# Causal attention, 32 heads of 16: value products of four heads in one run, scores alternating with the maxima's pieces, and the maxima's mask on VectorE

## What is computed

```python
q = (x @ Wq.T + bq).reshape(b, l, h, hd).transpose(0, 2, 1, 3)   # b=2, l=1024, h=32, hd=16
k = (x @ Wk.T + bk).reshape(b, l, h, hd).transpose(0, 2, 1, 3)
v = (x @ Wv.T + bv).reshape(b, l, h, hd).transpose(0, 2, 1, 3)
scores = jnp.einsum('bhqd,bhkd->bhqk', q, k) / math.sqrt(hd)
scores = jnp.where(jnp.tril(jnp.ones((l, l), bool)), scores, -jnp.inf)
att = jax.nn.softmax(scores, axis=-1)
out = jnp.einsum('bhqk,bhkd->bhqd', att, v)
```

## Time and profile before

| | us |
|---|---|
| median of three runs | 4538.52 |
| profiled execution, its own time | 4516.65 |
| span of the profiled execution | 4514.9 |
| TensorE busy / VectorE busy | 4124.7 / 2840.9 |
| ScalarE busy / GpSimd busy | 1448.6 / 1940.0 |
| mean granted TensorE clock, share of full speed | 0.929 |

### The profile page before, as it was taken

One profiled execution on the slowest core, in us unless ns is written; L12 is line 12 of the kernel. 1 busy time (PEld: TensorE's weight loads), 2 busy tenths in 40 slices (PEclk: granted clock), 3 DMA queues, 4 the chain that ended last, 5 costly groups with the idle time before them and its releaser, 6 DMA issues.

```text
span 4514.9 us, 60472 instructions
## 1 busy us (share of the span) xinstructions
PE 4124.7 (91%) x18820; PEld 2878.9 (64%) x18820; DVE 2840.9 (63%) x4778; ACT 1448.6 (32%) x2386; POOL 1940.0 (43%) x1951
## 2 busy tenths in 40 slices
PE   7999979969999999989779999799699999999797
PEld 5443457747777777767654434677477777777676
DVE  3545444458888888874444553444588888888744
ACT  1233421143444444332113333211434444443321
POOL 1111233246666666654311111332466666666543
PEclk9888989979999999999988888899799999999999
DMA  2211011010011100001121210110100111010011
GB/s 69 34 34 29 13 36 42 21 35 27 26 33 33 30 28 28 22 18 42 39 70 34 34 29 13 36 42 21 36 29 24 33 33 30 28 30 23 16 42 40
DMA packets 80968, 145.11 MB, mean 32 GB/s; under 512 B 16152, under 2 KB 18056, under 8 KB 80784
## 3 DMA queue, kind: packets, MB, share of 16 engines
q1 hardware_dynamic: 80784, 142.84, 12.0%
HBM read 112.64 MB, written 4.19 MB: 26 GB/s over the span
## 4 chain that ended last, share of the span: by engine, by line
PE 70%; issue 10%; DVE 9%; POOL 4%; ACT 3%; DVEq 2%; POOLq 1%; SPq 1%; DMA 0%; ACTq 0%
PE banks L489 13%; PE banks L490 12%; PE banks L491 12%; PE banks L671 7%; PE banks L654 4%; PE banks L626 4%; PE banks L833 4%; DVE conv L1327 3%; PE banks L826 2%; PE banks L844 2%; PE banks L630 2%; PE banks L533 1%; POOL wg_lo L1589 1%; ACT conv L1004 1%; DVEq L1330 1%
## 5 line engine op out<-in xcount | busy, mean ns | idle before, releaser
L1224 DVE TENSOR_REDUCE mx<-banks 128x1 f32<-128x512 f32 (+3 forms) x768 | 408.2, 555 | 333.2 <-PE banks L630 225.1
L1327 DVE SCALAR_TENSOR_TENSOR conv<-banks,cpar,conv 128x509 f32<-128x509 f32 (+2 forms) x576 | 428.1, 744 | 88.1 <-ACT conv L1004 73.1
L1564 POOL TENSOR_SCALAR_AFFINE_SELECT probs<-probs 128x256 f32<-128x256 f32 x256 | 103.9, 407 | 802.2 <-ACT probs L947 800.7
L947 ACT ACTIVATE probs<-banks 128x1024 f32<-128x1024 f32 (+3 forms) x384 | 295.5, 809 | 476.5 <-PE banks L654 475.9
L1162 DVE TENSOR_TENSOR Y<-banks,Y 128x512 f32<-128x512 f32 x400 | 275.6, 692 | 232.4 <-PE banks L491 232.2
L626 PE MATMUL banks<-stack_k,stack_q 48*128 48x512 f32 (+3 forms) x768 | 344.9, 475 | 19.6 <-DMA stack_k<-part_hi 9.4
L1480 POOL TENSOR_SCALAR f_hi<-f_raw 128x512 fp32r<-128x512 f32 x150 | 93.6, 624 | 582.5 <-PE banks L491 472.3
L671 PE MATMUL banks<-probs,V 128*17 128x512 f32 (+3 forms) x1536 | 339.5, 561 | 0.7 <-POOL probs L1564 0.5
L626 PEld LDWEIGHTS banks<-stack_k,stack_q 48*128 48x128 f32 x768 | 152.0, 207 | 293.7 <-DVE mx L1224 172.7
L489 PE MATMUL banks<-xhi,f_hi 128*128 128x512 f32 x800 | 328.6, 411 | 3.6 <-DVE xlo L1133 3.6
L489 PE MATMUL banks<-xhi,wx_hi 128*128 128x512 f32 x768 | 312.4, 407 | 14.2 <-DVE conv L1327 14.2
(11 more groups left out here) (205 smaller groups left out, 9982.9 us busy)
## 6 DMA issues: line engine op xcount, KB each, us to landing
m_raw<-in_w_mamba SPq DMA_DIRECT2D x224, 256.0 KB, 2.7
f_raw<-in_w_ffn SPq DMA_DIRECT2D x50, 768.0 KB, 4.6
stack_q<-part_hi SPq DMA_DIRECT2D x128, 64.0 KB, 2.4
stack_k<-part_hi SPq DMA_DIRECT2D x128, 64.0 KB, 2.5
X<-in_x SPq DMA_DIRECT2D x4, 1024.0 KB, 6.5
wqk_raw<-in_w_attn SPq DMA_DIRECT2D x8, 512.0 KB, 3.6
stack_q<-part_lo SPq DMA_DIRECT2D x64, 64.0 KB, 2.4
stack_k<-part_lo SPq DMA_DIRECT2D x64, 64.0 KB, 2.4
```

The lines of the kernel that those rows point to most:

```text
L947: act.activation(probs[n % 2][:, 2 * p:2 * p + 2, 0:w], banks[:, 2 * p:2 * p + 2, 0:w], ACT.Exp, scale=1.0 / HD ** 0.5).then_inc(exp_done[ ...
L1224: dve.tensor_reduce(mx[:, s, h * TT + i:h * TT + i + 1], bank[RING_BANKS[ring % 3]][:, 0:cols], AX.X, ALU.max).then_inc(ring_free, 1)
L1327: r = dve.scalar_tensor_tensor(out=rest, in0=src[:, 0:HALF - lag], scalar=cpar[:, o:o + 1], in1=rest, op0=ALU.mult, op1=ALU.add)
```

## The change

The scores of a step are issued head by head with one piece behind each, and the values of the step before are one item of four heads behind the fourth piece (`values`, one wait for both pairs). The mask product on TensorE goes. In its place VectorE reads the piece with one instruction that adds `mask_qk` (now fp32, 128 x 512, zero but for its last 128 columns), writes the sum back to the bank and keeps the maximum. `mask_qk` is built by GpSimd at the start of each batch's attention.

```diff
                 for n in range(NS):
-                    for q in range(4):
-                        if q < 2:
-                            yield "scores", t, n, q
-                        elif n > 0:
-                            yield "values", t, n - 1, q - 2
+                    for q in range(QUAD):
+                        yield "score", t, n, q
...
+                    if n > 0:
+                        yield "values", t, n - 1
...
-                for q in range(2):
-                    yield "values", t, NS - 1, q
+                yield "values", t, NS - 1
...
-                        if diag:
-                            r = pe.matmul(dst[:, cols - P:cols], ident_b[:], mask_qk[:], start=False, stop=True,
-                                          skip_group_check=True)
...
-                        pe.wait_ge(exp_done[p], START + it)
-                        for h in (2 * p, 2 * p + 1):
-                            dst = bank[h]
-                            r = pe.matmul(dst[:, 0:HALF - lo],
+                        if h % 2 == 0:
+                            pe.wait_ge(exp_done[h // 2], START + it)
+                        r = pe.matmul(bank[h][:, 0:HALF - lo],
...
-                        for h in (2 * p, 2 * p + 1):
+                        for p in range(2):
+                            if j * P >= s * HALF:
+                                pe.wait_ge(masked[p], b * (NQ * TT) + (t * TT + j + 1))
+                            else:
+                                pe.wait_ge(exp_done[p], START + it + 1)
+                        for h in range(QUAD):
...
+                        if diag:
+                            held(dve, ring_done, b * RING + ring + 1)
+                            dve.tensor_tensor_reduce(out=src, in0=src, in1=mask_qk[:, HALF - cols:HALF], scale=1.0,
+                                                     scalar=NEG, op0=ALU.add, op1=ALU.max, accum_out=col
+                                                     ).then_inc(ring_free, 1)
+                        else:
+                            dve.wait_ge(ring_done, b * RING + ring + 1)
+                            dve.tensor_reduce(col, src, AX.X, ALU.max).then_inc(ring_free, 1)
...
+                pool.memset(mask_qk[:], 0.0)
+                pool.drain()
+                pool.affine_select(out=mask_qk[:, HALF - P:HALF], in_=mask_qk[:, HALF - P:HALF],
+                                   compare_op=ALU.is_ge, fill=NEG, base=0, pattern=[[-1, P]],
+                                   channel_multiplier=1).then_inc(mask_built, 1)
```

More of the change, by code:

```diff
@@ L640, in _ @@
                         ring += 1
-                    elif what == "scores":
-                        t, n, p = arg
+                    elif what == "score":
+                        t, n, h = arg
                         s, j = STEPS[n]
@@ L646, in _ @@
                         it = b * (NQ * NS) + (t * NS + n)
[L647 removed]
+                        if n == 0 and h == 0 and t % 2 == 0 and t < 4:
                             pe.wait_ge(ones_rows, b * (16 * 8) + 16 * 4 * (t // 2 + 1))
[L649 removed]
+                        if n == 0 and h == 0:
                             pe.wait_ge(mt_in, START + (b * NQ + t + 1) * 32)
[L651 to L658 removed]
+                        if h % 2 == 0:
+                            pe.wait_ge(exp_done[h // 2], START + it)
+                        r = pe.matmul(bank[h][:, 0:HALF - lo],
+                                      stack_k[buf][base:base + ROWS + 2, h, j * P:(j + 1) * P],
+                                      stack_q[buf][base:base + ROWS + 2, h, s * HALF + lo:(s + 1) * HALF],
+                                      start=True, stop=True)
+                        if h % 2:
+                            r.then_inc(st_done[h // 2], 1)
                     elif what == "values":
[L660 removed]
+                        t, n = arg
                         s, j = STEPS[n]
@@ L938, in _ @@
                         ring += 1
-                    elif what == "scores":
-                        t, n, p = arg
+                    elif what == "score" and arg[2] % 2:
+                        t, n, p = arg[0], arg[1], arg[2] // 2
                         s, j = STEPS[n]
@@ L1221, in _ @@
                         t, n = arg
-                        h, i, s, cols, _ = PIECES[n]
-                        dve.wait_ge(ring_done, b * RING + ring + 1)
-                        dve.tensor_reduce(mx[:, s, h * TT + i:h * TT + i + 1], bank[RING_BANKS[ring % 3]][:, 0:cols],
-                                          AX.X, ALU.max).then_inc(ring_free, 1)
+                        h, i, s, cols, diag = PIECES[n]
+                        src, col = bank[RING_BANKS[ring % 3]][:, 0:cols], mx[:, s, h * TT + i:h * TT + i + 1]
+                        if diag:
[6 more added lines that the diff above has]
+                            dve.tensor_reduce(col, src, AX.X, ALU.max).then_inc(ring_free, 1)
                         ring += 1
@@ L1242, in _ @@
                     elif what == "values":
-                        t, n, p = arg
+                        t, n = arg
                         s, j = STEPS[n]
-                        if p == 1 and j == CPH * (s + 1) - 1:
+                        if j == CPH * (s + 1) - 1:
                             dve.wait_ge(pv_done, b * (NQ * NS) + (t * NS + n) + 1)
@@ L1457, in _ @@
             pool.memset(half_neg[:], -0.5)
-            for m, v in ((ident, 0.0), (ident_b, 0.0), (mask_qk, 0.0), (quarter, 0.25)):
+            for m, v in ((ident, 0.0), (quarter, 0.25)):
                 pool.memset(m[:], v)
```

26 lines of the change are left out of this document (6 added, 20 removed).

## The result

The changed kernel takes 4367.84 us (median of four runs, 4359.74 to 4379.33), the kernel before 4529.14 us beside it: a ratio of 0.965, 95% interval 0.961 to 0.969. Faster, as forecast; the time lies inside the range, 34 us above the 4334 us predicted. The profiled execution took 4379.33 us with a span of 4377.6, so the span fell by 137.3 us where the sum had 182.

The account below looks back on a forecast made before the run. VectorE was to replace TensorE as bound: 28.6 + 5.8 + 3.6 = 38.0 us a quad, 51.2 with projections, 292.4 a batch plus 18 for half clock; 182 us less in both batches, 4334 us, range 4230 to 4450.

Parts of the forecast that it names:

- The bound moves to VectorE: Attention's middle quads: TensorE's need falls from 47.7 to 25.9 us, below VectorE's 28.57, so VectorE becomes the bound.
- Values, masks, pieces on TensorE: Each quad at full clock: TensorE saves 8.7 us on values, 5.1 on masks, 8 on pieces running beside scores.
- The fused instruction's 5.8 us a quad: On VectorE, add-and-max with its second instruction costs 0.18 us extra a piece, 5.8 us for 32 pieces.
- Idle of 3.6 us a quad: VectorE idles 0.3 us a step around the values, 3.6 us a quad; ends 0 and 14.5 us.
- Half clock: Quads 0 to 6: if 117 us at half clock stay, they add 18 us, making 310 us a batch.
- Quads with projections, 51.2 us: Quads 1 and 3 at full clock: projections add about 11.2 us and the GpSimd wait two, to 38.0 us.
- Start, quad 7 and the rest: 0: Attention's start, quad 7 and phases outside the attention: no change, at most 1 us a batch for GpSimd's mask.
- The clock stays down: Rival: quads 0 to 6 stay at low clock, 48 us each, 69 with projections; 4470 us; chance 0.10.
- Better: Rival: 0.06 us extra, 1.5 us idle a quad, clock up; quads of 32.0 and 45.2 us, 4215 us; chance 0.15.
- dear: Rival: fused instruction at its upper end, 18.6 us a quad, 4478 us; at the middle, 0.38 us, 4398; chance 0.10.
- lockstep: Rival: scores stand behind pieces waiting for banks, VectorE idles 14.5 us a quad; 4450 us; chance 0.12.
- slower: Rival: VectorE's diagonal pieces pay an unoverlapped fixed price, 1.0 us extra; quads 64.2 and 77.4 us, 4667 us; chance 0.05.

Follow-up runs that it names:

- A: The kernel before with scores alternating with pieces, values in halves and masks on TensorE: 4453.15 us, ratio 0.983.
- A, V: The changed kernel with the mask product back on TensorE and a plain reduction for all pieces: 4463.13 us, ratio 0.982.
- the run with short reads: The changed kernel with VectorE reading only 128 columns of every piece and no mask applied: 4273.76 us, ratio 0.944.
- V alone: The kernel before with the values of four heads in a row at each step's end, masks and score pairs as before: 4548.36 us, ratio 1.003.
- all four kernels with V: The kernels with four heads' values together, with or without fused mask and alternation, the changed kernel among them: ratios 1.003, 0.978, 0.982 and 0.965.

## Why the prediction was right, and where it was not

**The bound moves to VectorE.** Right in part. At full clock, cutting VectorE's reads took the quad from 32.5 us (estimate) to 28.7. "VectorE busy for over 85%" of quad 5 did not come, it was 28.32 of 39.23 us, 72%, because that quad was at 0.74; in the full-clock stretch shown it is 83%. TensorE is busy for 92% there, just over the 90% that the prediction had called a sign of being wrong. And in the time at half clock, 131 of 306 and 191 of 323 us, TensorE was the bound. "Clock at 1.00 for two thirds" didn't come either.

**Values, masks, pieces on TensorE.** Right. Values x8 at 1.05 us at full clock; 7.2 us a quad between A and A, V, for a term of 8.7. Masks: 40.3 for 47 (estimate), 6.7 us for 5.1. Scores and pieces whose rows lie on different halves start together (277.10 twice). The pieces of quad `t + 2`, on the rows of the scores, take turns with them, as the prediction had it: score, piece, score, piece, score start at 356.84, 357.00, 357.23, 357.29 and 357.57 us. TensorE's need of 25.9 us was 27.2 in the run with short reads.

**The fused instruction's 5.8 us a quad.** The term of the quad's sum that failed by most. The smallest VectorE instruction (175 ns) was added to each of 32 pieces as if it stood behind the first. The follower takes 142 ns but starts with the next instruction. What is left is 0.02 us at 512 columns, some 0.5 us a quad. The lower end, "0 extra", was the nearer one. Being two instructions does not mean being paid twice: a fused one and its follower take 0.60 us to the next start (267.56 to 268.16). The "0.92 ns a column" of the reductions is 1.04 by the groups of the kernel before (689 ns at 512 columns, 289 at 128); no term was worked out from it.

**Idle of 3.6 us a quad.** About right: 32.5 less 28.2 leaves 4.3 (an estimate, as the 32.5 is).

**Half clock.** The error that hid the first one. The prediction kept 117 us of it at a cost of 18 us a batch. It was 131 and 191 us, and each us costs more than the 0.16 assumed. Four quads without projections, as length and half-clock time: 36.7 and 14, 39.3 and 20.4, 41.1 and 27, 42.1 and 32 us. The slope over all eight such quads (2, 4, 5 and 6 of each batch) is about 0.31, which makes 41 and 59 us a batch; the line meets no half clock at 32.5. The prediction had set 45 us for a quad wholly at half clock on one wholly VectorE-bound at 38; by this line it is 47 on 32.5. So the quads' 310 us came out as 305.7 and 322.8 by luck, from two errors of opposite sign: 32.5 for 38, some 27 us a batch too much, and 41 to 59 for 18, some 23 to 41 too little.

**Quads with projections, 51.2 us.** 57.26 and 58.79 in the first batch, both at 0.85; with 0.31 us for each of their 17 half-clock us they would be 52 and 53. The term holds at full clock. The wait for GpSimd grew from 1.65 to 3.0 us in quad 3.

**Start, quad 7 and the rest: 0.** Wrong, and this is the miss in the total: 37 us. Quad 7 "stays" in its instructions, but not in its clock: 45.5 us where the clock fell within it, 33.0 where it didn't. The start had been balanced by masks that left TensorE and went to VectorE; its extra came with a lower clock, in kernels with and without the fused instruction. What lowers it there was not found.

**The rivals.** "The clock stays down" for all of quads 0 to 6 did not happen in the changed kernel, but did nearly in V alone, 357 us of half clock in a batch of 434; it had half of the truth, and 0.10 was too little for a low clock that all four kernels with V show in part (322 to 657 us of both batches). Its levels are known here as clock columns of 1.00 and 0.50 alone, and waits in every step are not what it needs: a quad of V alone, with TensorE busy for 54.68 of its 54.68 us, was granted 0.59. "Better" had the full-clock quad right, 32.0 us, but its 4215 us leave out the 18 us of half clock a batch that the forecast carries, as do the times of "dear", "lockstep" and "slower". (The middle case of "dear" also adds up to 4388 us, not 4398.) "Dear", "lockstep" and "slower" are excluded by 708 ns and by waits of 2.6 us a quad. What spoke for "lockstep" does show: a piece waits 0.45 us for VectorE and starts at 279.71, and the score behind it at 279.72.

## What to carry to other kernels

Price a change in TensorE's columns at both clocks: here the part that saved the most columns (7 us of a 43 us quad) bought nothing alone, since the time at half clock grew with it, while moving small mask products to a VectorE instruction that reads the data anyway bought 2.5%. When a part must be valued, build each part alone and each one undone; in one run of all three the sum would have been credited to the wrong one. And phases whose instructions don't change can still be granted another clock (quad 7 took 33.0 and 45.5 us in the two batches of one execution), so they don't cost "0" by right.

## What the runs showed of the hardware

- The add-and-max with an accumulator on VectorE, fp32, one operand in PSUM and one in SBUF and the sum written back to PSUM: 708 ns for 512 columns, 566 for 384, 299 for 128, against 685, 551 and 289 for the plain reductions (the 289 and the 551 from the kernel before). Its second instruction takes 142 ns, beside the next one.
- Values of four heads together: 1.05 us at full clock for x8, as long as x4. Kernels with this order were at half clock (a granted clock of 0.50) for 322 to 657 us of both batches' quads, those without for 93 to 248. One with an always busy TensorE was granted 0.59 over 54.68 us, and 512 more columns a step lowered the half-clock time by only a fifth (322 to 257 us). No run here separates what sets the clock.
- One product of 32 columns between two pairs of values cost 0.34 us from its start to the next at full clock, about 4 us a quad.
- A us at half clock costs less than a us: about 0.31 us of length for each in the changed kernel's quads, 0.41 in those of the kernel before (estimates, slopes over eight quads each). With the fused mask alone a quad of 40.3 us took 66.9 at a clock of 0.51.
